# Attention of a fused two-layer kernel: scores between a pair's two turnings, returned rows taken in halves, deviations one tile at a time, a first tile alone, and the last two layernorms as one chain

## The reference

```
x = x + fp8_product(layernorm(x), ctx)              # quantised product with the context
x = x + moe0(layernorm(x))                          # 32 experts, top 4, shared expert
x = x + attention(layernorm(x), ctx, ctx, gamma)    # 8 heads; this block is what changes
x = x + moe1(layernorm(x))                          # 8 experts, top 2, shared expert
```

```
qk  = einsum('dq,dl->ql', q_head, k_head) / sqrt(32)     # 256 x 256 scores
ret = einsum('ql,dl->dq', softmax(qk, axis=-1), v_head)  # 32 x 256
x   = x + gamma * ret
```

## Time and profile before

| | |
|---|---|
| time, median of 3 runs | 440.56 us (438.98 to 441.39) |
| the profiled execution | 440.37 us, span 438.6 us |
| busy in the span | PE 79%, DVE 60%, ACT 44%, POOL 38% |
| attention stage | from about 241 us to 333 us |

### The profile page before, as it was taken

One profiled execution on the slowest core, in us unless ns is written; L12 is line 12 of the kernel. 1 busy time (PEld: TensorE's weight loads), 2 busy tenths in 40 slices (PEclk: granted clock), 3 DMA queues, 4 the chain that ended last, 5 costly groups with the idle time before them and its releaser, 6 DMA issues.

```text
span 438.6 us, 8046 instructions
## 1 busy us (share of the span) xinstructions
PE 344.7 (79%) x2303; PEld 193.1 (44%) x2303; DVE 264.1 (60%) x733; ACT 195.2 (44%) x453; POOL 167.1 (38%) x274
## 2 busy tenths in 40 slices
PE   0003397789999999999998268678865799999897
PEld 0001274534544545445445145445544444444354
DVE  3998859535555555555554967565567745555274
ACT  1341245255555555555541257677742155554010
POOL 2000302376666766666631023222030266773200
PEclk9999998899999999999999556698996799999999
DMA  8999990076232222334644798000002023231341
GB/s 237 377 284 298 350 252 3 7 237 192 89 99 91 90 92 92 97 92 109 188 155 149 278 280 200 10 0 1 2 1 96 24 85 97 95 90 59 109 168 48
DMA packets 28295, 57.30 MB, mean 131 GB/s; under 512 B 3806, under 2 KB 12734, under 8 KB 28254
## 3 DMA queue, kind: packets, MB, share of 16 engines
q1 hardware_dynamic: 20110, 37.85, 28.3%
q0 software_dynamic: 6528, 17.83, 13.2%
q10 hardware_dynamic: 1616, 1.11, 0.9%
HBM read 44.72 MB, written 12.06 MB: 129 GB/s over the span
## 4 chain that ended last, share of the span: by engine, by line
PE 66%; DVE 20%; issue 6%; ACT 3%; POOL 3%; DMA 2%; DVEq 0%; SPq 0%; ACTq 0%; POOLq 0%
PE bank L1299 21%; PE bank L1328 13%; PE bank L1310 5%; PE bank L1178 5%; PE bank L1290 4%; DVE x_sb L971 3%; PE bank L1389 2%; PE bank L1377 2%; DVE st L731 2%; PE bank L1217 2%; PE bank L1191 2%; DVE att_nm L1002 2%; DMA x_sb<-x 2%; PE bank L1408 1%; PE bank L1145 1%
## 5 line engine op out<-in xcount | busy, mean ns | idle before, releaser
L1299 PE MATMUL bank<-arena,xT 128*64 x272 | 111.2, 491 | 1.1 <-ACT xT L630 1.1
L1302 PE MATMUL bank<-xn,xT 128*64 128x384 f32 (+1 forms) x272 | 111.2, 491 | 0.0
L515 POOL DMA_INDIRECT xg<-m_xn,tab x68 | 66.2, 973 | 64.7 <-PE bank L1290 31.3
L504 POOL DMA_INDIRECT m_ys<-ysb,dest x68 | 67.3, 989 | 38.7 <-DVE ysb L943 22.0
L1328 PE MATMUL bank<-arena,hT 96*64 (+1 forms) x272 | 70.5, 381 | 2.6 <-DVE hT L929 2.4
L1331 PE MATMUL bank<-xn,hT 96*64 96x256 f32 (+1 forms) x272 | 70.6, 381 | 0.0
L623 ACT ACTIVATE xn<-arena 128x768 f32 (+1 forms) x68 | 56.3, 828 | 21.9 <-issue 21.8
L955 DVE TENSOR_TENSOR hh<-sg,bank 128x192 f32<-128x192 f32 (+1 forms) x71 | 24.8, 350 | 60.1 <-ACT sg L646 60.1
L1328 PEld LDWEIGHTS bank<-arena,hT 96*64 96x64 f32 (+1 forms) x272 | 34.7, 135 | 39.9 <-issue 29.5
L630 ACT ACTIVATE xT<-bank 128x256 f32<-128x256 f32 x71 | 27.3, 384 | 48.5 <-PE bank L1290 47.7
L923 DVE COPY xn<-arena 96x512 f32 (+1 forms) x68 | 29.2, 429 | 23.8 <-issue 23.8
(11 more groups left out here) (179 smaller groups left out, 548.1 us busy)
## 6 DMA issues: line engine op xcount, KB each, us to landing
arena<-w_gu SPq DMA_DIRECT2D x3, 3456.0 KB, 19.4
arena<-w_dn SPq DMA_DIRECT2D x3, 1728.0 KB, 26.0
arena<-m_ys SPq DMA_DIRECT2D x8, 512.0 KB, 5.8
arena<-w_gu SPq DMA_DIRECT2D x2, 1408.0 KB
m_xn<-xn SPq DMA_DIRECT2D x2, 1024.0 KB, 7.3
arena<-m_ys SPq DMA_DIRECT2D x8, 256.0 KB, 3.7
arena<-w_dn SPq DMA_DIRECT2D x2, 704.0 KB
arena<-w_gu SPq DMA_DIRECT2D x1, 1152.0 KB, 11.7
```

The lines of the kernel that those rows point to most:

```text
L504: nc.gpsimd.indirect_dma_start(out=ys_d[L.name], out_offset=bass.IndirectOffsetOnAxis(ap=dest[:, s:s + 1], axis=0), in_=ysb[:, s % BUFS, : ...
L515: nc.gpsimd.indirect_dma_start(out=xg[:, b, :], out_offset=None, in_=xn_d[L.name], in_offset=bass.IndirectOffsetOnAxis(ap=d["tab"][:, s:s ...
L1299: T.matmul(bank[2 + s % 2][0:BLOCK, 0:2 * J2], xT[:, s % 2, c, 0:BLOCK], arena[:, bass.ds(off + c * 2 * J2, 2 * J2)], start=(c == 0), stop ...
L1302: return T.matmul(bank[2 + s % 2][BLOCK:P, 0:2 * J2], xT[:, s % 2, c, BLOCK:P], gu2[:, s % 2, cols], start=(c == 0), stop=(c == C - 1), ti ...
```

## The change

In `chains` every query tile from 1 on gets a chain of its own, tile 1 among them; the three chains for the next layer keep two tiles each, at other g. Tile 0's queries are computed first and alone. ScalarE waits for GpSimd's first chain before it normalises tile 1, between the exponentials of head 2 and the copy of head 0. A tile's returned rows are summed in two halves of two instructions, at g % 4 == 0 and g % 4 == 2, tile 3 to tile 7 in the loop. The reciprocals stand at g % 4 == 2 ahead of `head_max(g+4)`. On TensorE the scores of pair p+2 stand between the two turnings of pair p; the spreading of the inverses is a function of its own, called after odd pairs, one pair ahead of the products with the values. The first router rows of the next layer are turned between the last two turnings. The layernorms of tiles 6 and 7 become one, behind `tile_out(7)`.

```diff
-        chains = [(-1, (2, 3), True, 2), (2, (4, 5), True, 7), (7, (6, 7), True, 12),
-                  (11, (0, 1), False, 15), (19, (2, 3), False, 23), (27, (4, 5), False, 31)]
+        chains = [(-2, (1,), True, -1), (-1, (2,), True, 2), (2, (3,), True, 6), (6, (4,), True, 10), (10, (5,), True, 14),
+                  (14, (6,), True, 18), (18, (7,), True, 22),
+                  (20, (0, 1), False, 24), (23, (2, 3), False, 28), (27, (4, 5), False, 31)]
...
             act.wait_ge(chain_ready, 1)
-            for t in range(2):
-                normalise(t, q_ready)
+            normalise(0, q_ready)
             for g in range(3):
                 softmax_exp(g)
+            act.wait_ge(rstd_ready, 1)
+            normalise(1, q_ready)
...
-            def take(t):
-                combine(L0, t).then_inc(x2_ready, 1)
-                dve.wait_ge(x2_ready, t + 1)
+            def take(t, half=None):
+                if half != 1:
+                    dve.wait_ge(*returned(L0, t))
+                for k in range(L0.K) if half is None else range(half * 2, half * 2 + 2):
+                    V.scalar_tensor_tensor(out=x_sb[:, t, :], in0=back_rows["m0"][:, t, k, :],
+                                           scalar=small["m0"]["rw"][:, t, k:k + 1], in1=x_sb[:, t, :],
+                                           op0=ALU.mult, op1=ALU.add).then_inc(x2_ready, 1)
+                    dve.wait_ge(x2_ready, t * L0.K + k + 1)
...
             take(0)
+            queries([0])
             take(1)
-            queries([0, 1])
-            take(2)
-            take(3)
             statistics(chains[0][1]).then_inc(stats_ready, 1)
             for g in range(4):
                 head_max(g)
-
-            takes = {1: 4, 2: 5, 6: 6, 7: 7}
+            take(2)
+            statistics(chains[1][1]).then_inc(stats_ready, 1)
+
             for g in range(nheads):
-                if g in takes:
-                    take(takes[g])
+
+                t, h = divmod(g + 12, HPT)
+                if t < NT and h == 0:
+                    take(t, 0)
+                elif t < NT and h == 2:
+                    take(t, 1)
+                if g % HPT == 2:
+                    head_inverses(g // HPT)
...
                 if g + 4 < nheads:
                     head_max(g + 4)
-                if g % HPT == HPT - 1:
-                    head_inverses(g // HPT)
...
-            layernorm([NT - 2], last_ready)
             tile_out(NT - 1)
             dve.wait_ge(x3_ready, NT)
-            layernorm([NT - 1], last_ready)
+            layernorm([NT - 2, NT - 1], last_ready)
...
             for p in range(nheads // 2):
                 turn_p(2 * p)
-                turn_p(2 * p + 1)
                 if p + 2 < nheads // 2:
                     scores(p + 2)
-                if p >= 2 and p % 2 == 0:
+                elif p == nheads // 2 - 1:
+                    pe.wait_ge(p_raw, 2 * (nheads - 3))
+                    turn_rows(L1, 0)
+                turn_p(2 * p + 1)
+                if p % 2 == 1:
+                    inverses(p // 2)
+                elif p >= 2:
                     values(p // 2 - 1)
             pe.wait_ge(p_raw, 2 * (nheads - 2))
-            turn_rows(L1, 0)
             values(NT - 1)
```

More of the change, by code:

```diff
@@ L1391, in turn_p, with inverses @@
                 ins.then_inc(tp_done, 1)
-            def values(t):
+            def inverses(t):
                 pe.wait_ge(inv_ready, t + 1)
@@ L1402, in values @@
                                  tile_position=(0, h * HEAD))
+            def values(t):
                 pe.wait_ge(pT_ready, HPT * (t + 1))
```

## The result

The changed kernel takes 422.85 us, the median of 4 runs (418.97 to 425.27), against 440.52 us before (4 runs, 438.98 to 441.39): a ratio of 0.957, 95% interval 0.952 to 0.961. The ratio leaves out the run of 425.27 us, which counts as slow; the median of the other three is 421.41. The forecast was 426, range 420 to 433. The profiled execution took 424.28 us, its span being 422.5.

A forecast was written before the change was run, and what follows sets the result against it. Handovers between engines, a ring of VectorE, ScalarE and TensorE waits, were taken to bound the attention stage. Start 2.2, loop 10.2 and end 2.3 us make 14.7; 440.37 - 14.7 = 425.7, forecast 426 us, range 420 to 433.

The forecast's parts named there:

- The start: Up to pair 2's scores: first maximum 4.9 us earlier, of which 2.2 us arrive after ScalarE's wait for GpSimd.
- rival E: Waits on GpSimd's one-tile chains eat the gain; loop at 8.0 us a tile, start's gain lost: 438 to 441; chance 0.04.
- The loop: Attention tiles at full clock: busiest engine sets the pitch, 6.8 us a tile while sums last, then 6.4; gain 10.2 us.
- The end: Pair 15's scores to last normalise: one joint layernorm for tiles 6 and 7, 15.2 us against 17.5; gain 2.3 us.
- rival D: Attention stage: VectorE instructions with two SBUF inputs lose up to 0.15 us each to GpSimd; 3.6 us, 429; chance 0.05.
- A (old pitch): Loop: the ring keeps 7.9 us a tile because VectorE's order still stalls it; 6.3 us later, 432; chance 0.15.
- C (half clock throughout): Attention stage: clock stays at half, TensorE limits at 10.9 us a tile; slower, 450; chance 0.04.
- B, the clock back at once: From 255.3 us, TensorE without a gap: 13 us of half-clock work become about 8.5; 421; chance 0.11.

The follow-up runs named there:

- e10: Changed kernel with all of TensorE's old order: scores behind both turnings, inverses spread at the head of values, reciprocals at g % 4 == 3; 426.4 us.
- e1: Changed kernel with the scores of pair p+2 behind both turnings of pair p again; 423.2 us.
- e2: Changed kernel with each tile's returned rows summed in one piece of four instructions instead of two halves; 424.4 us.
- e5: Changed kernel with the layernorms of tiles 6 and 7 separate again, tile 6's ahead of tile_out(7); 426.1 us.
- e3: Changed kernel with tiles 0 and 1 getting their queries together on VectorE again, tile 2's sums staying behind the first maxima; 424.0 us.
- e8: Kernel before with only TensorE's new order: scores between the turnings, inverses spread one pair ahead, reciprocals early; 432.9 us, ratio 0.982.
- e7: Changed kernel with the reciprocals at g % 4 == 3 behind the maximum and their spreading at the head of values; 428.1 us.
- e4: Changed kernel plus eight unread TensorE products: five ahead of the first scores, three between turning 0 and pair 2's scores; 418.8 us.
- e12: Changed kernel plus ten unread TensorE products: seven ahead of the first scores, three between turning 0 and pair 2's scores; 418.3 us.
- e6: Changed kernel with tiles 0 and 1 getting queries together, plus five unread TensorE products ahead of the first scores; 424.3 us.

## Why the prediction was right, point by point

**The start.** Close in each mark: pair 2's scores at 255.38 (255.3 forecast), pair 4's at 264.39 (264.5), pair 5's at 269.76 (269.7), head 10's maximum at 270.93 (270.9), the first maximum at 249.57 (248.9), ScalarE's wait for GpSimd 1.5 us (about 2). That the marks of the pairs agree to 0.1 is in part luck: the stage began 0.48 us later, and they came 0.4 to 0.6 earlier after its beginning than forecast, so the gain at pair 2 is 2.6 and not 2.2. GpSimd's chain has 16 instructions by its trace and not the 17 that the text counts; of the forecast only rival E's bound of 8.0 us hangs on it, which would be 7.5. That TensorE at half clock is the limit from there, so that its order is worth nothing, is borne out by 14.4 us from pair 2 to pair 5 in the changed kernel and in e10 alike, and by 12.0 in e1 against 12.2 in e2 and e5. What the text left open, e3 showed: none of the gain is due to the first tile being alone.

**The loop.** This is the term that was mis-sized: 12.1 us gained, 10.2 forecast. It accounts for the whole surplus, as the end of the stage moved by 16.5 us (332.80 to 316.27) with 14.7 forecast. The median lies another 1.4 us below the profiled run, inside the spread. The pitch was 6.8 and then 6.4 forecast from VectorE's work, 6.25 on average measured (31.24 us for five tiles). VectorE's maxima of heads 10, 14, 18 and 22 start at 270.93, 277.45, 283.98 and 290.51, 6.53 apart, so its work was nearly right (6.65). But the scores in that time start at 269.76, 275.81 and 281.85, 6.05 apart: TensorE, without a gap in these rows, was the limit (6.3 forecast), and VectorE fell behind it by 0.5 a tile, out of the slack that the two pairs in flight give. From 285 VectorE is on the chain, from 293 ScalarE; head 26's maximum comes only 5.3 behind head 22's. So the pitch that the largest sum of work sets came only once the slack was used up, and here that took two of the five tiles.

The reason for the loop's gain was right but incomplete. The prediction gave it to the scores' earlier start and to the sums in halves; these are worth 1.6 and 0.8 us in e1 and e2, each against a kernel that has the rest of the change. The bulk, 8 to 9 us of the 12.2 from pair 2 to pair 15, went with the first of either order (e8, e10): the stall that the earlier trace rows show, and with it the two returns to half clock. In the kernel before TensorE stood idle for 3.61 us from 275.52, the clock fell at 277.4 and the work from 279.13 to 284.2 ran at half clock; the second time the clock fell at 304.7, behind 1.42 us of idle time at 302.68, and was back at 308.1. TensorE was busy for about 5 and 3.4 us at half clock; by the rows at either level (turnings 1.97 for 1.09, values 1.93 for 1.07) about half of that, some 4 us, is what the clock cost. This is an estimate, and takes it that all of it delayed the end.

**The end.** 15.3 us from pair 15 (15.2 forecast) against 17.5 before. The prediction gave the 2.3 us to the joint layernorm, and e5, which takes it out of the changed kernel, finds 2.4. But e7 takes out the early reciprocals and finds 1.9, and the two can't both be parts of 2.2. The other runs settle it: with the joint layernorm and late reciprocals the end takes 17.5 (e10) and 17.2 (e7), with early reciprocals and two layernorms 17.4 (e8) and 17.6 (e5). Either alone is worth next to nothing (0.3 us at most), both together 2.2. The rows of the kernel before say why: tile 7's reciprocals were late there as well, but the layernorm of tile 6 stood behind them and covered the wait for the values, so that tile 7's output followed without one:

```profile
324.98 0.19 DVE L1009 RECIPROCAL arena<-arena 128x8 f32<-128x8 f32 x1
328.17 0.48 DVE L1013 TENSOR_SCALAR arena<-bank,gamma_sb 128x256 f32<-128x256 f32 x1
```

Without that layernorm the wait lies open, 1.67 us in e7. The prediction's step had the values of tile 7 in time, so its sum came out; that the early reciprocals are its condition it did not say.

**Contention the other way, rival D.** Four sums under GpSimd's chain took 2.03 us at 251.98, those of tile 1 without it 2.04, and the sums of the loop 0.97 to 1.01 a half. VectorE loses nothing in these rows. The rule of the Trainium skill, page "SBUF — State Buffer", section "Who interferes with whom", that whoever issues first blocks the other, shows on GpSimd's side alone here (0.42 to 0.45 us for 0.19).

**The other rivals.** A (old pitch) and C (half clock throughout) did not come. E's waits for GpSimd were 1.5 us at tile 1 and 2.6 in all for VectorE. E's price was wrong in its own terms: a loop of five tiles at 8.0 us is 6.8 longer than the forecast's, and with the 2.2 of the start that gives 435 us, not 438 to 441, so E too would have been faster than before by over 2.2 us. B, the clock back at once, did not come in the changed kernel, and its price was right when it was forced: 4.5 us forecast, 4.1 and 4.5 measured in e4 and e12, at 418.8 and 418.3. They beat both kernels.

**What stays open.** No run undoes the chains of one tile by themselves, or the first router rows between the last two turnings, so their share is not shown. Each kernel was profiled once.

## What to carry to other kernels

In a ring of engines, look first for the longest pile on one engine and for the stretch in which TensorE stops behind it. Here either of two reorderings across that stretch removed most of the loss, and the second added 2.9 to 4.3 us (7.9 and 9.3 alone, 12.2 together). Mark the same few instructions in every profile and compare the stretches between them: these repeated to 0.2 us where the runs of one kernel spread over 6. Choose the marks so that a stretch that pays for another is in the sum. Undo each part of a change by itself: here one of five, the first tile alone, was worth nothing. And try each part by itself on the old kernel too: undone one by one, the joint layernorm and the early reciprocals looked worth 2.4 and 1.9 us, and together they are worth 2.2.

## What the runs showed of the hardware that was not expected

TensorE's clock came back at different moments in the same work. The changed kernel, e1 and e2 had TensorE busy without a gap from 257 to 264 at half clock; in e1 and e2 it returned at 264.5 and 265.5, as in e5 at 264.0, in the changed kernel at 269.0. The changed kernel and e5 have the same instructions up to the end of the attention, and both were busy throughout these 5 us, first the changed kernel, then e5:

```profile
264.00:269.00 5.00, 5.00 (x31) 2.56 (x29) 2.37 (x6) 2.96 (x10) 0.98 (x5) 0.50 0.87 262
```
```profile
264.00:269.00 5.00, 5.00 (x49) 3.11 (x52) 3.39 (x8) 4.61 (x16) 1.28 (x7) 1.00 0.85 249
```

This is worth 2.2 to 2.4 us (12.0 to 12.2 against 14.4 from pair 2 to 5), with nothing in the order of instructions to account for it in e5. The clock also goes with the changed kernel's spread between runs: the mean granted clock of its four runs is 0.962 at 418.97 us, 0.955 at 421.41, 0.952 at 424.28 and 0.944 at 425.27. In which stage the others lost it was not profiled. e4, which left the half clock earlier, spread over 0.8 us, but e12 over 3.2.

And the clock fell at 250.2 in e4, where TensorE had been idle twice for 2.0 us since 245, at 249.4 in e6, behind 4.3 us of idle time, and at 313.3 in the changed kernel with TensorE busy in every microsecond from 310 to 315, on logits with eight columns and the first held product.
